# Splitting the convolution's input for tiles 7 to 15: VectorE's subtraction replaced by an accumulating transfer on GpSimd's queue

## What is computed

```python
# x (32, 64, 1024); conv: 4 groups of 16 channels, 9 taps, padding 4
h = conv(x, weight) + einsum('nd,od->no', cond, c_weight)[:, :, None] + bias[None, :, None]
q = einsum('bsd,rd->bsr', h, Wq_w)                 # 16 values per row
scores = einsum('bsr,er->bse', q, keys)            # 64 experts
top_vals, top_idx = top_k(scores, 16)
gate = sum(one_hot(top_idx) * softmax(top_vals)[..., None], axis=-2)
z = einsum('bsd,nd->bsn', h, A_w)                  # 512 = 64 experts x rank 8
out = einsum('bsn,on->bso', z * gate_per_expert, B_w) * 2.0
return x + out
```

## Time and profile before

| | |
|---|---|
| median of 3 runs | 240.22 us |
| the profiled execution, its own time | 240.4 us |
| its span in the profile | 238.6 us |
| granted TensorE clock | 1.0 of full speed in all 40 slices |
| TensorE matmuls | busy 223.9 us (94%) |
| VectorE | busy 198.5 us (83%) |
| ScalarE | busy 128.9 us (54%) |
| GpSimd | busy 7.2 us (3%) |
| DMA queue of SyncE | 40.55 MB, 52.1% of 16 engines' span |

### The profile page before, as it was taken

How to read it: one execution, slowest core, us unless ns; L and a number is a source line. 1 busy time by engine, 2 the same in 40 slices (tenths; PEclk the granted TensorE clock), 3 DMA queues, 4 the chain that set the end, 5 groups by cost and what they waited for, 6 DMA issues and landing times.

```text
span 238.6 us, 4043 instructions
## 1 busy us (share of the span) xinstructions
PE 223.9 (94%) x1345; PEld 198.1 (83%) x1345; DVE 198.5 (83%) x449; ACT 128.9 (54%) x322; POOL 7.2 (3%) x16
## 2 busy tenths in 40 slices
PE   8999999999899976996979999899989999999995
PEld 6998998988879865884878989798888989898884
DVE  2799989999798897988998899898998897786542
ACT  4996767363483734636477474736377455352100
POOL 2010080000000000000000000000000000000000
PEclk9999999999999999999999999999999999999999
DMA  6996065869726334253164454754354154538552
GB/s 204 377 403 240 15 221 167 312 191 308 230 106 214 100 98 167 89 135 88 44 199 168 122 176 135 212 165 153 87 195 171 38 176 131 177 93 300 174 186 91
DMA packets 24869, 40.89 MB, mean 171 GB/s; under 512 B 2832, under 2 KB 11920, under 8 KB 24848
## 3 DMA queue, kind: packets, MB, share of 16 engines
q1 hardware_dynamic: 24704, 40.55, 52.1%
q10 hardware_dynamic: 144, 0.08, 0.1%
HBM read 28.04 MB, written 12.58 MB: 170 GB/s over the span
## 4 chain that ended last, share of the span: by engine, by line
DVE 51%; PE 28%; issue 11%; ACT 4%; DMA 3%; SPq 1%; DVEq 0%; POOL 0%; ACTq 0%; POOLq 0%
DVE x_lo L1095 7%; PE p_z L888 7%; DVE h_lo L1095 6%; DVE h_t L1137 6%; DVE x_blk L1119 4%; DVE zt_lo L1095 3%; DVE a_raw L1266 3%; DMA a_raw<-in_b_w 3%; DVE a_lo L1095 2%; DVE bt_lo L1095 2%; DVE a_raw L1198 2%; PE p_conv L837 1%; PE p_out L937 1%; PE p_out L929 1%; DVE sc_b L1249 1%
## 5 line engine op out<-in xcount | busy, mean ns | idle before, releaser
L509 ACT ACTIVATE h_hi<-h_t 128x1024 fp32r<-128x1024 f32 x16 | 17.0, 1064 | 40.7 <-DVE h_t L1137 40.7
L888 PEld LDWEIGHTS p_z<-a_hi,h_hi 128*128 128x128 f32 x240 | 32.6, 188 | 2.6 <-issue 0.6
L888 PE MATMUL p_z<-a_hi,h_hi 128*128 128x264 f32 x240 | 34.0, 284 | 0.2 <-DVE a_raw L1266 0.2
L888 PE MATMUL p_z<-a_hi,h_lo 128*128 128x264 f32 x240 | 34.0, 284 | 0.0
L888 PE MATMUL p_z<-a_lo,h_hi 128*128 128x264 f32 x240 | 34.0, 284 | 0.0
L888 PEld LDWEIGHTS p_z<-a_hi,h_lo 128*128 128x128 f32 x240 | 31.1, 188 | 0.0
L888 PEld LDWEIGHTS p_z<-a_lo,h_hi 128*128 128x128 f32 x240 | 31.1, 188 | 0.0
L1095 DVE TENSOR_TENSOR x_lo<-x_blk,x_hi 128x1536 fp32r<-128x1536 f32 (+4 forms) x18 | 25.2, 1406 | 1.5 <-ACT x_hi L509 1.5
L559 ACT ACTIVATE p_conv<-p_conv,u 128x128 f32<-128x128 f32 x88 | 23.6, 356 | 1.7 <-PE p_conv L837 1.4
L509 ACT ACTIVATE x_hi<-x_blk 128x1536 fp32r<-128x1536 f32 (+4 forms) x18 | 22.1, 1226 | 2.3 <-DMA x_blk<-in_x_blocks 1.2
L1095 DVE TENSOR_TENSOR h_lo<-h_t,h_hi 128x1024 fp32r<-128x1024 f32 x16 | 19.2, 1201 | 0.0
(11 more groups left out here) (160 smaller groups left out, 436.7 us busy)
## 6 DMA issues: line engine op xcount, KB each, us to landing
x_nat<-in_x_rows SPq DMA_DIRECT2D x16, 512.0 KB, 5.0
out_dram<-x_nat SPq DMA_DIRECT2D x31, 256.0 KB, 3.2
x_blk<-in_x_blocks SPq DMA_DIRECT2D x14, 516.0 KB, 3.6
z_dram<-a_raw SPq DMA_DIRECT2D x64, 64.0 KB, 1.8
a_raw<-z_dram SPq DMA_DIRECT2D x16, 256.0 KB, 2.8
a_raw<-in_a_wq SPq DMA_DIRECT2D x8, 264.0 KB, 6.1
x_nat<-in_b_w SPq DMA_DIRECT2D x4, 512.0 KB, 8.8
a_raw<-in_b_w SPq DMA_DIRECT2D x3, 512.0 KB, 4.1
```

The source lines that it names most:

```text
L509: nc.scalar.activation(dst, src, ACT.Copy).then_inc(s, 1)
L888: mm = nc.tensor.matmul(z_bank(t, b)[:, 0:HB], h[:, t % 2, r, :], a[:, r, b * HB:(b + 1) * HB], start=k == 0 and r == 0, stop=k == 2 and r ...
```

## The change

For tiles 7 to 15 (`XD = 7`), ScalarE writes the negated rounded value, -fp32r(x), into `x_lo` (`negate_x`), and a transfer issued by GpSimd adds x to it in place (`accum_op=ALU.add`), which leaves x - hi. VectorE's `split_x` stays for tiles 0 to 6. What is moved beside that: x is prepared one step earlier (`split_x(i + 4)`, `differ(i + 4, ·)`, `load_blocks(i + 5)`), with tile 8 as an extra one in step 4; the load of x now stands behind `z_in`, not ahead of it; ScalarE's `split_z34` and `split_z22` come ahead of `split_h`; VectorE's `split_bt` comes a step later (for sums 0, 1 and 3); and VectorE's `split_h` is behind `split_q`, where it was between `turn_q` and `split_q` in odd steps.

```diff
+XD = 7
...
         def x_lo_done(t, half=1):
+            if t >= XD:
+                return s_xld[t % 2], 16 * ((t - XD) // 2 + 1)
             return s_xlo, x_split_count(t, half)
...
                 z_out(i)
-                if i + 4 < NT:
-                    load_blocks(i + 4)
+                if i == 3:
+                    load_blocks(7)
                 z_in(i)
+                if i + 5 < NT:
+                    load_blocks(i + 5)
...
+            for t in range(XD, NT):
+                pool.wait_ge(s_xneg, t - XD + 1)
+                pool.dma_start(x_part(x_lo[:, t % 2], t, 1), x_raw(t, 1), accum_op=ALU.add).then_inc(s_xld[t % 2], 16)
...
+            def negate_x(t):
+                nc.scalar.activation(x_part(x_lo[:, t % 2], t, 1), x_raw(t, 1), ACT.Copy, scale=-1.0).then_inc(s_xneg, 1)
...
-                if i + 3 < NT:
+                if i < 5:
                     split_x(i + 3)
+                elif i + 4 < NT:
+                    split_x(i + 4)
...
+                if FP + 3 <= i < NT - 1 and i % 2:
+                    split_z34(m)
+                    split_z22(m)
...
                 if i + 2 < NT:
                     split_h(i + 2)
-                if FP + 3 <= i < NT - 1 and i % 2:
-                    split_z34(m)
-                    split_z22(m)
+                if i == 4:
+                    negate_x(7)
+                    split_x(8)
+                    negate_x(8)
+                elif 5 <= i < NT - 4:
+                    negate_x(i + 4)
+                if TB <= i < TB + 4:
+                    split_bt(i - TB)
...
-                if i + 3 < NT:
+                if i < 5:
                     differ(i + 3, 0)
+                elif i + 4 < NT:
+                    differ(i + 4, 0)
...
-                if i + 3 < NT:
-                    split_x(i + 3)
+                if i == 3:
+                    split_x(6)
...
+                if i - TB in (1, 2, 4):
+                    split_bt(i - TB - 1)
                 if TB <= i < TB + 4:
                     sum_b(i - TB)
...
+                if i == 4:
+                    differ(8, 0)
+                    differ(8, 1)
                 if i in (4, 6):
                     sum_w(i // 2)
                 if TS <= i + 1 < NT - 1:
                     turn_q(i + 1)
-                if i == FP + 2:
-                    sum_z4(0)
-                elif i >= FP + 4 and i % 2 == 0:
+                if i <= FP + 1:
+                    add(i - 2, 0)
+                elif i == FP + 2:
+                    add(FP - 1, 1)
+                elif i % 2 == 0:
                     add_22(m)
-                    sum_z4(m + 1)
-                elif i + 2 < NT:
-                    split_h(i + 2)
+                elif i < NT - 1:
+                    add_11(m)
                 if TS <= i + 1 < NT - 1:
                     split_q(i + 1)
                 if i >= FP + 2 and i % 2 == 0:
-                    if i + 2 < NT:
-                        split_h(i + 2)
+                    sum_z4((i - FP - 2) // 2)
+                if i + 2 < NT:
+                    split_h(i + 2)
+                if i >= FP + 2 and i % 2 == 0:
                     split_z12((i - FP - 2) // 2)
```

More of the change, by code:

```diff
@@ L193, in adaln_ffn @@
         s_xd = sem("s_xd")
+        s_xneg = sem("s_xneg")
+        s_xld = [sem(f"s_xld{k}") for k in range(2)]
         s_ws = sem("s_ws")
@@ L752, in _ @@
                     split_h(i + 2)
-                if FP + 3 <= i < NT - 1 and i % 2:
-                    split_z34(m)
-                    split_z22(m)
+                if i == 4:
[6 more added lines that the diff above has]
+                    split_bt(i - TB)
                 if i >= FP + 2 and i % 2 == 0:
                     split_z12((i - FP - 2) // 2)
-                if TB <= i < TB + 4:
-                    split_bt(i - TB)
                 if FP + 3 <= i < NT - 1 and i % 2:
@@ L1399, in _ @@
                 m = (i - FP - 3) // 2
-                if i + 3 < NT:
+                if i < 5:
                     differ(i + 3, 0)
+                elif i + 4 < NT:
+                    differ(i + 4, 0)
                 copy_scores(i)
                 top_first(i)
-                if i + 3 < NT:
+                if i < 5:
                     differ(i + 3, 1)
+                elif i + 4 < NT:
+                    differ(i + 4, 1)
                 take_first(i)
@@ L1428, in _ @@
                     split_ws(i // 2)
-                if i <= FP + 1:
-                    add(i - 2, 0)
                 if i == FP + 1:
                     split_z1(0)
+                if i - TB in (1, 2, 4):
+                    split_bt(i - TB - 1)
                 if TB <= i < TB + 4:
@@ L1438, in _ @@
                     split_z22(m)
-                    add_11(m)
                 if i == FP + 2:
                     sum_z31(0)
-                    add(FP - 1, 1)
                     sum_z2(0)
@@ L1461, in _ @@
                 if i >= FP + 2 and i % 2 == 0:
-                    if i + 2 < NT:
-                        split_h(i + 2)
+                    sum_z4((i - FP - 2) // 2)
+                if i + 2 < NT:
+                    split_h(i + 2)
+                if i >= FP + 2 and i % 2 == 0:
                     split_z12((i - FP - 2) // 2)
-                if TB <= i < TB + 4:
-                    split_bt(i - TB)
+                if i == TB + 2:
+                    split_bt(2)
                 if FP + 3 <= i < NT - 1 and i % 2:
```

## The result

The change takes **267.28 us** (median of 4 runs, 265.80 to 268.37) against 240.24 for the kernel before in the same job: a ratio of 1.112, with a 95% interval of 1.107 to 1.118. The forecast was 243.5 us with a range up to 250. The direction was right, the size was not.

A forecast was written before the change was run, and what follows sets the result against it. VectorE was taken to bound the kernel. Terms for steps 3 to 11, -1.1 + 2.35 - 0.6 + 0.2 + 1.05 + 1.3 + 0.4 = +3.6, 0.3 less at the scores, took the profiled 240.4 to 243.7, median 243.5 us; range 235.8 to 250.

The forecast's parts named there:

- What bounds the kernel: The chain of waits runs through VectorE for half of the span, though busy shares say TensorE.
- TensorE's floor: TensorE's own work per pair of steps, 12.33 and 13.86 us; 26.2 would do, against VectorE's 26.9.
- The load's wait: Steps 6 to 11: x's load behind z_in idles VectorE before the next reduction; chance 0.60, 240.7 to 250 us.
- the landing: Time from issue of x's load to its arrival: taken as 3.9 us, between 3.2 and 5.9.
- The sensitivity of 4.8 us: Each us of landing is paid in steps 6 to 10, some 4.8 in all.
- The transfer is in time: Accumulating transfer has 12.5 us, needs between 5.1 and 15; conv_sum asks for the result after some 20.5.
- No wait for GpSimd's transfer: Sign expected in the profile after: nothing waits for the accumulating transfer.
- the +2.35 us of step 4: Extra passes ahead of tile 5's query bring the next reduction to 16.65 us against 14.31.
- Step 5: VectorE loses the subtraction (1.6 us) and gains a second bt_lo (1.1): -0.6 us.
- That TensorE sets the pace: Rival: late x does not hold VectorE, steps 7 to 12 go at 13.86 and 12.33; 236.2 us, chance 0.30.
- The late transfer: Rival: at 15 us, TensorE or SyncE waits 2.5 us on each of nine tiles; 266 us, chance 0.05.

The follow-up runs named there:

- e3: The changed kernel without the accumulating transfers (x not added to x_lo) and with the load of x ahead of z_in; 236.97 us, ratio 0.984.
- e2: The changed kernel without the accumulating transfers, x_lo holding only the negated half; load of x still behind z_in; 247.41 us, ratio 1.028.
- e6: The changed kernel with GpSimd's transfer made a plain copy of the same bytes at the same place, load behind z_in; 248.85 us, ratio 1.034.
- e8: The changed kernel, load ahead of z_in, passes of tiles 7 and 8 moved, x earlier only from step 5, transfer from tile 8; 235.59 us, ratio 0.980.
- e1: The changed kernel with only the load of x (tiles 9 to 15) issued ahead of z_in again, transfer kept; 240.97 us, ratio 1.001.

## Why the prediction was right or wrong

**What bounds the kernel: right.** The chain was put on VectorE, with TensorE's floor at 12.33 and 13.86 us for a pair of steps. With the load ahead, e3 shows TensorE busy without a gap from 140 to 200 us, and its scores follow each other by 12.18 and 13.57 us: my floor was a little too high.

**The load's wait: right in mechanism and place, wrong in size.** The load stands right behind z_in's issue, L1141 is waited for, and q_c is ahead of h_lo, as forecast. Even in the change itself the load goes out when the chain says: 9.86, 10.55 and 8.54 us after the reduction in steps 7, 8 and 9, against 9.85, 10.5 and 8.6 predicted. For the kernel without the transfer, where the landing is 4.0 us and I had taken 3.9, the chain holds step by step, to 0.6 us: 16.12, 14.15, 15.60, 13.44, 15.61 and 12.21 measured for steps 6 to 11, against 16.05, 14.40, 15.05, 13.15, 15.05 and 12.30 predicted.

**The term that failed is the landing.** "I take 3.9 ... since only 256 KB stand ahead of it." What stands ahead of it is also the accumulating transfer, issued 2 us earlier, and the landing is 7.4 us (6.1 to 8.0). I named 5.9 as the bound from above, from loads beside plain loads, and cut even that from the range by stopping at 5.2. The sensitivity of 4.8 us for each us of landing was about right: 3.4 us more landing than in e2 cost 14.4 us in steps 6 to 10, where 4.8 times 3.4 is 16.3. VectorE's waits were 5.0, 6.3 and 6.8 us in the even steps from 6 to 10 and 4.1 in step 7, not 2 to 3 and little.

The page "DMA: Bandwidth & Descriptors" of the Trainium skill, section "Issuing engines are not separate DMA queues", spoke for a slow load in the text, beside the rows of x_nat in pairs, and the trace agrees with its rule: GpSimd's transfer slows SyncE's load at the same place from 4.0 (e2) to 7.4 us. But the rule does not give the size. As a neighbour like any other it would do what e6's copy does: a landing of 4.4 us and 248.9 us in all. That is near the 249 which I wrote beside the rule, though there it came from a landing of 5.1. That the accumulation takes 2.1 times the engines' time is in no row of the kernel before, and I priced the transfer only for its own lateness, never for what it does to others. I did have the upper bound in hand (15 us for the transfer, by twice the work on the destination) and used it only for the rival that the transfer itself comes late.

**The transfer is in time: wrong for its first tile.** The text gave it 12.5 us of slack, because TensorE asks for the low half 20.5 us into a step. That holds for tiles that are negated one step ahead. Tile 7 is negated in step 4 and asked for in that same step, about 10 us after its reduction: TensorE waited 4.6 us, the load of tile 9 was held up with it, and VectorE waited 6.6 us for that. Step 4 was 23.48 us instead of the 16.66 predicted, 6.8 us more. "No wait for GpSimd's transfer" was false in this one place. Where the transfer is absent, the +2.35 us of step 4 holds nearly exactly (16.80), and so does its chain: in e2 the query comes 14.0 us into the step, and I had 13.9.

**Step 5: off by 1.7 us** where the stall of step 4 does not cover it (16.33 in e2). I counted the removed subtraction and the added bt_lo, and did not see that VectorE's w_lo comes first: in e3 it waits 1.58 us for ScalarE's w_hi, which is behind x_hi, and that one waits 3.52 us for TensorE's product (VectorE, then ScalarE). A removal upstream only let VectorE reach that wait sooner. This is read from the trace; no run takes that wait away.

```profile
90.55 0.42 DVE L1116 TENSOR_TENSOR w_lo<-h_c,w_hi 128x256 fp32r<-128x256 f32 x1 [1.58 <-ACT w_hi L519]
```

```profile
88.20 1.49 ACT L519 ACTIVATE x_hi<-x_blk 128x1536 fp32r<-128x1536 f32 x1 [3.52 <-PE p_conv L858]
```

**How it adds up.** Predicted 243.5. The transfer-free kernel of e2 is 247.4: 3.9 us are errors of my chain, 3.0 of them in steps 4 to 11 and 1.7 of those in step 5. The transfer adds 19.9 by the medians. The two profiled executions of the table lie 21.0 apart (246.4 and 267.4), and their steps differ by 6.7 in step 4, 14.4 in steps 6 to 10 and 2.0 in step 11, less the 1.7 that step 5 gets back, which is 21.4. Had I written 7.4 for the landing, the sum would have given about 260, and with tile 7's stall of 6.8 about 267. That this meets the measured time is partly luck: it takes 16.8 us for the landing, more than the 14.4 that the table shows, and lacks the 3.0 us by which my chain was short.

**The rivals.** That TensorE sets the pace was false for this change, but it is what the design can do: e3's 237.0 and e8's 235.6 lie near the 236.2 that this rival gave. Part of that is luck: it put the scores of tile 7 1.1 us earlier than before, and in e3 they come 0.9 later (110.65 against 109.73), while the six steps from there take 77.4 us and not 78.6. The late transfer, with a chance of 0.05, gave 266 and came near the measured number for the wrong reason, by luck: only one tile's transfer was waited for, not nine. What I missed is the rival between the two: a transfer that is in time itself and makes another one late.

## What to carry to other kernels

When a change adds a transfer, do not only ask whether it arrives in time; find the transfer with the least slack on the same DMA engines, and price that one beside it. Look too at which of the two is issued first: 2 us behind the transfer the load took 7.5 us, 2 us ahead of it 3.6. An issue that stands behind another's wait in a queue is a hidden due time: here its place alone was worth 10 to 13 us without the new transfer and 26 with it. And where work is moved one step earlier, look at the first step apart, since it carries a tile twice: moving that step from 4 to 5 was worth 2.8 us (238.4 to 235.6), and moving it on to 7 gave them back and 1.1 more (239.5).

## What the runs showed of the hardware

- An accumulating transfer within SBUF (f32 onto fp32r) cost the DMA engines twice what a copy without change of type did: 9 times 768 KB took 39.3 us of all 16 engines against 18.4, its landing was 6.7 us against 3.8, and GpSimd's issue 0.87 us against 0.53. A load of 516 KB issued 2 us behind it landed in 7.4 us, behind the copy in 4.4, with no such neighbour in 3.4 to 4.0. SyncE's own issue of that load took 1.17 to 1.20 us in steps 6, 8 and 10 of the change, and 0.38 in every one of these steps in e2.
- Issued 1.5 to 2.2 us ahead of the accumulating transfer, the same load landed in 3.4 to 3.8 us (e1); issued 0.2 us ahead of it, in 6.1 (step 9 of the change).
- TensorE's granted clock fell after it had run dry, and the fall outlasted the wait: 0.54 from 162 to 166 us, where it had work throughout, so a stall of VectorE cost TensorE once as idling and once more as slower work. Over the span the clock was 0.942 in the change and 0.985 in e8_shift5, and TensorE's busy time for the same 1345 matmuls 233.9 against 224.5 us. How much of the 27 us is this was not measured apart.
